# Folding projection weights head by head on 64 rows of TensorE, in a decoder block on one core

## The reference

```python
x = x + mixer(layernorm(x))          # gated mixer, 256 wide, a causal filter over the 4 batches
x = x + xattn(layernorm(x), ctx)     # cross attention, 16 heads of 64, relu features of size 128
x = x + ffn(layernorm(x))            # 8 experts, each token goes to 2 of them

def xattn(query_input, source_input, Wq, Wk, Wv, Wo, proj):
    q = einsum('bld,dhk->blhk', query_input, Wq)
    k = einsum('bld,dhk->blhk', source_input, Wk)
    v = einsum('bld,dhk->blhk', source_input, Wv)
    qp = relu(einsum('blhd,md->blhm', q, proj) / sqrt(128)) + 1e-3
    kp = relu(einsum('blhd,md->blhm', k, proj) / sqrt(128)) + 1e-3
    kvs = einsum('blhm,blhd->bhmd', kp, v)
    num = einsum('blhm,bhmd->blhd', qp, kvs)
    den = einsum('blhm,bhm->blh', qp, kp.sum(axis=1))
    return einsum('blhd,hdk->blk', num / den[..., None], Wo)
```

## Time and profile before

| | us |
|---|---|
| median of 3 runs | 284.33 |
| lowest and highest | 284.23, 286.0 |
| the profiled execution, its own time | 283.41 |
| span of the profiled execution | 281.6 |

### The profile page before, as it was taken

The page is one execution under the profiler, slowest core; times in us unless marked ns, Lnnn a source line. Parts: engine busy times, 40 slices in busy tenths (PEclk is TensorE's granted clock), DMA queues, the critical chain, the costliest instruction groups (busy, mean ns, idle before and its releaser), DMA issues.

```text
span 281.6 us, 5724 instructions
## 1 busy us (share of the span) xinstructions
PE 250.0 (89%) x1697; PEld 214.2 (76%) x1697; DVE 190.6 (68%) x713; ACT 163.9 (58%) x343; POOL 123.7 (44%) x183
## 2 busy tenths in 40 slices
PE   7799999999999999999998999896799989999700
PEld 4558677676888999879887998775699989999600
DVE  4868759587868888998889889899367222232215
ACT  3566466564677777667766776661156656565400
POOL 5648999651001002047103701270236777777710
PEclk9999999999999999999999999999699999999975
DMA  7999999930012000001000100019557579984147
GB/s 208 276 240 202 204 205 195 198 47 2 0 58 94 0 0 3 1 21 48 9 3 17 52 11 3 9 55 280 155 160 198 160 211 281 354 256 130 43 181 266
DMA packets 38446, 34.05 MB, mean 121 GB/s; under 512 B 3581, under 2 KB 31234, under 8 KB 38288
## 3 DMA queue, kind: packets, MB, share of 16 engines
q1 hardware_dynamic: 35312, 28.96, 43.4%
q0 software_dynamic: 2272, 4.24, 4.4%
q10 hardware_dynamic: 832, 0.49, 0.6%
HBM read 19.80 MB, written 14.32 MB: 121 GB/s over the span
## 4 chain that ended last, share of the span: by engine, by line
PE 59%; DVE 20%; DMA 8%; SPq 5%; issue 4%; POOL 2%; ACT 1%; DVEq 0%; POOLq 0%; ACTq 0%
PE bank L1250 10%; PE num L1175 10%; DVE X L913 8%; PE bank L1136 5%; PE num L1260 5%; PE num L1114 5%; DMA xb<-dispatched 3%; PE num L245 3%; PE num L247 3%; PE bank L245 3%; PE num L246 3%; PE bank L1078 3%; PE bank L246 2%; PE bank L247 2%; DMA wo_sb<-in_wo 2%
## 5 line engine op out<-in xcount | busy, mean ns | idle before, releaser
L913 DVE SCALAR_TENSOR_TENSOR X<-num,rden,X 128x128 f32<-128x128 f32 x256 | 72.1, 344 | 6.6
L1175 PEld LDWEIGHTS num<-kvw_sb,q 128*128 128x128 f32 x512 | 65.9, 190 | 12.0 <-ACT q L574 5.7
L1175 PE MATMUL num<-kvw_sb,q 128*128 128x130 f32 x512 | 68.7, 277 | 3.6 <-DVE X L913 3.6
L657 ACT ACTIVATE relu_z<-bank 128x512 f32<-128x512 f32 x64 | 38.1, 596 | 21.6 <-PE bank L247 21.5
L537 POOL DMA_INDIRECT dispatched<-rows,slot_i x32 | 31.3, 977 | 40.4 <-DVE rows L979 31.6
L557 POOL DMA_INDIRECT expert_out<-yo,xb x39 | 38.1, 977 | 20.1 <-ACT yo L686 11.3
L1013 DVE TENSOR_TENSOR hid<-bank,silu_g 128x256 f32<-128x256 f32 x39 | 16.5, 424 | 41.2 <-ACT silu_g L682 41.2
L574 ACT ACTIVATE q<-relu_z 128x512 f32<-128x512 f32 x64 | 40.4, 632 | 6.7 <-DVE acc L832 0.8
L1250 PE MATMUL bank<-xT,wgu_sb 128*128 128x128 f32 x312 | 43.3, 284 | 0.2 <-ACT xT L574 0.2
L1250 PEld LDWEIGHTS bank<-xT,wgu_sb 128*128 128x128 f32 x312 | 39.8, 200 | 0.5 <-issue 0.5
L245 PE MATMUL bank<-y2T_hi,feat_hi 128*128 128x512 f32 x64 | 30.4, 475 | 0.2
(11 more groups left out here) (170 smaller groups left out, 403.2 us busy)
## 6 DMA issues: line engine op xcount, KB each, us to landing
wgu_sb<-in_wgu SPq DMA_DIRECT2D x39, 256.0 KB, 3.4
dispatched<-pad_row SPq DMA_DIRECT2D x3, 2795.0 KB, 32.6
xb<-dispatched SPq DMA_DIRECT2D x39, 65.0 KB, 3.5
y_back<-expert_out SPq DMA_DIRECT2D x4, 512.0 KB, 4.9
wd_sb<-in_wd SPq DMA_DIRECT2D x1, 1024.0 KB, 4.7
out<-X SPq DMA_DIRECT2D x4, 256.0 KB, 2.4
X<-in_x SPq DMA_DIRECT2D x3, 256.0 KB, 5.9
expert_out<-yo,xb POOLq DMA_INDIRECT x39, 3.5
```

The costliest lines, as they stand in the source:

```text
L657: a.activation(relu_z[:, k % 2, :], z_bank[k % 2], ACT.Relu).then_inc(relu_done, 1)
L913: v.scalar_tensor_tensor(tile_of(n, t), banks[:, t // 2, t % 2, 0:P], rden[:, h % 2, t:t + 1], tile_of(n, t), ALU.mult, ALU.add).then_inc( ...
L1175: nc.tensor.matmul(num[:, 2 * (h % 2) + t // 2, HA * (t % 2):HA * (t % 2 + 1)], q[:, h % 4, part], kvw_h, start=True, stop=True).then_inc( ...
```

## The change

The pairs are taken apart. `projT_sb` and `wo_sb` become 128 columns wide and have no zero blocks, so that the four memsets and `apart` go. Each head is folded by a matmul of its own, on rows 0 to 63 or 64 to 127 (`row_half`), with 128 moving columns. The host lays out wk, wv, wq and wo anew: the heads of group g lie on rows 0 to 63 when g is even and on rows 64 to 127 when g is odd. In the folds of the start PE goes over two groups at once, in turns from the one half of the rows to the other and from one bank to the other. In the batches' `project` all four heads of a group lie on the same half of the rows and go to the same bank. wo is loaded by two transfers, with 512 contiguous floats to a row.

```diff
-            projT_sb = sa("projT_sb", [P, 2 * M])
+            projT_sb = sa("projT_sb", [P, M])
-            wo_sb = sa("wo_sb", [P, H // 2, 2 * P])
+            wo_sb = sa("wo_sb", [P, H // 2, P])
+        def row_half(g):
+
+            return slice(DH * (g % 2), DH * (g % 2 + 1))
             for i in range(2):
                 part = slice(G * i, G * (i + 1))
                 sp.dma_start(wv_sb[:, part, :], wv[:, part, :]).then_inc(ld_wvo[i], 16)
-                sp.dma_start(wo_sb[0:DH, part, 0:P], wo[0:DH, part, :]).then_inc(ld_wvo[i], 16)
-                sp.dma_start(wo_sb[DH:P, part, P:2 * P], wo[DH:P, part, :]).then_inc(ld_wvo[i], 16)
+                sp.dma_start(wo_sb[:, part, :], wo[:, part, :]).then_inc(ld_wvo[i], 16)
             act.dma_start(projT_sb[0:DH, 0:M], projT).then_inc(ld_proj, 16)
-            act.dma_start(projT_sb[DH:P, M:2 * M], projT).then_inc(ld_proj, 16)
+            act.dma_start(projT_sb[DH:P, 0:M], projT).then_inc(ld_proj, 16)
-            v.memset(projT_sb[0:DH, M:2 * M], 0.0).then_inc(apart, 1)
-            v.memset(projT_sb[DH:P, 0:M], 0.0).then_inc(apart, 1)
-            v.memset(wo_sb[0:DH, :, P:2 * P], 0.0).then_inc(apart, 1)
-            v.memset(wo_sb[DH:P, :, 0:P], 0.0).then_inc(apart, 1)
             def project(ps, w, g):
-                for i in range(G // 2):
-                    last = nc.tensor.matmul(ps[:, 2 * M * i:2 * M * (i + 1)], w[:, G // 2 * g + i, :], projT_sb[:, :],
-                                            start=True, stop=True)
+                for i in range(G):
+                    last = nc.tensor.matmul(ps[:, M * i:M * (i + 1)], w[row_half(g), G * (g // 2) + i, :],
+                                            projT_sb[row_half(g), :], start=True, stop=True)
                 return last
             pe.wait_ge(ld_proj, 32)
-            pe.wait_ge(apart, 2)
-            for g in range(NG):
-                pe.wait_ge(ld_wk[g], 16)
-                project(fold_bank[g], wk_sb, g).then_inc(wk_full, 1)
-            pe.wait_ge(apart, 4)
-            for g in range(NG):
-                pe.wait_ge(ld_wvo[g // 2], 48)
-                pe.wait_ge(wk_lo_done, g + 1)
-                for i in range(G // 2):
-                    last = nc.tensor.matmul(fold_bank[g][:, 2 * P * i:2 * P * (i + 1)], wv_sb[:, G // 2 * g + i, :],
-                                            wo_sb[:, G // 2 * g + i, :], start=True, stop=True)
-                last.then_inc(wvo_full, 1)
+            for a in range(2):
+                for i in range(G):
+                    if i % 2 == 0:
+                        pe.wait_ge(ld_wk[2 * a + i // 2], 16)
+                    for g in (2 * a, 2 * a + 1):
+                        fold = nc.tensor.matmul(fold_bank[g][:, M * i:M * (i + 1)], wk_sb[row_half(g), G * a + i, :],
+                                                projT_sb[row_half(g), :], start=True, stop=True)
+                        if i == G - 1:
+                            fold.then_inc(wk_full, 1)
+            for a in range(2):
+                pe.wait_ge(ld_wvo[a], 32)
+                pe.wait_ge(wk_lo_done, 2 * a + 2)
+                for i in range(G):
+                    for g in (2 * a, 2 * a + 1):
+                        fold = nc.tensor.matmul(fold_bank[g][:, P * i:P * (i + 1)], wv_sb[row_half(g), G * a + i, :],
+                                                wo_sb[row_half(g), G * a + i, :], start=True, stop=True)
+                        if i == G - 1:
+                            fold.then_inc(wvo_full, 1)
```

More of the change, by code:

```diff
@@ L190, in decoder_kernel @@
         ld_wq = sem("ld_wq")
-        warm_set, apart = sem("warm_set"), sem("apart")
+        warm_set = sem("warm_set")
         ld_bias, ld_small, ld_biaso, ld_woa, ld_wd = map(sem, ("ld_bias", "ld_small", "ld_biaso", "ld_woa", "ld_wd"))
@@ L1294, with halves @@
     coef = np.concatenate([w["attn_zero"], w["attn_pos"][:, :NB - 1]], axis=1)
+    def halves(a):
+        return a.reshape(2, 2, G, DH, P).transpose(1, 3, 0, 2, 4).reshape(P, H // 2, P)
     arrays = {
@@ L1303 @@
         "coef": np.repeat(coef, MHD, axis=0).reshape(2, P, NB).transpose(1, 0, 2),
-        "wk": w["xattn_Wk"].transpose(1, 2, 0).reshape(H // 2, P, P).transpose(1, 0, 2),
-        "wv": w["xattn_Wv"].transpose(1, 2, 0).reshape(H // 2, P, P).transpose(1, 0, 2),
-        "wq": w["xattn_Wq"].transpose(1, 2, 0).reshape(H // 2, P, P).transpose(1, 0, 2),
-        "wo": w["xattn_Wo"].reshape(H // 2, P, P).transpose(1, 0, 2),
+        "wk": halves(w["xattn_Wk"].transpose(1, 2, 0)),
+        "wv": halves(w["xattn_Wv"].transpose(1, 2, 0)),
+        "wq": halves(w["xattn_Wq"].transpose(1, 2, 0)),
+        "wo": halves(w["xattn_Wo"]),
         "projT": w["xattn_proj"].T,
```

## The result

| | before | changed |
|---|---|---|
| median, us | 284.28 (4 runs) | 288.27 (4 runs) |
| lowest and highest | 284.21, 286.0 | 286.93, 290.12 |
| the profiled execution, its own time | 283.41 | 290.12 |
| its span | 281.6 | 288.4 |

The ratio is 1.0118, with a 95% interval from 1.0071 to 1.0165. Two later calls on chips of the same speed gave 1.0127 [1.0076, 1.0179] and 1.0155 [1.0094, 1.0216]. The change makes the kernel slower by 1.2 to 1.6%, 3.4 to 4.4 us. The forecast was 285.1 us, with a range to 287.2: wrong.

A forecast was written before the change was run, and what follows sets the result against it. The prediction took PE to bound the kernel from 13.44 us on, with the norm's work as late at the start. Start -0.05, wq matmuls +0.16 and row changes +0.64 gave +0.75: 284.33 + 0.75 = 285.1 us, range 283.6 to 287.2.

The forecast's parts named there:

- PE must empty before the change ... I take 0.08: Folds of wq: each change between whole array and half its rows costs 0.08 us, 8 x 0.08 = 0.64.
- The second rival: Folds of wq: PE empties at each change, 8 x 0.16 = 1.3 us, giving 285.7 us; chance 0.22.
- the join that cost nothing: Lower bound for a change of rows: kvw to the fold of wq today, 24.90 + 0.90 = 25.80, without loss.
- The +0.04 for the matmuls themselves: Each fold of wq: eight records, 0.90 us in place of 0.86; four times, +0.16 us.
- The memsets ... worth nothing: Start: the memsets ran while DVE waited for x, to 6.28 us, so dropping them gains nothing.
- x ... lands before wo does: Start: x of batch 0, issued by ACT, lands at 6.28 us, ahead of wo, and the change shortens nothing there.
- The first is there at about 8.8: Start: wo's first half lands at about 8.8 us in place of 9.26, through quicker transfers, 0.4 us each half.
- Against it: on the whole array loading runs beside the matmuls: Folds of wq: argument that weight loads stay hidden, since PE and PEld are both busy today.
- the third rival: Folds of wq: weight loads on the same half no longer hidden, +3.6 us, giving 288.7 us; chance 0.08.
- half way between the emptying and the dear end, 287.2: Top of the forecast range, set between PE emptying at each change (285.7 us) and 287.8 us.
- the dear end: Folds of wq: each change costs a full PE restart, 0.42 us, +3.5 us in all, giving 287.8 us; chance 0.05.
- The median lies 0.9 us above that execution: Whole kernel: carries the forecast from the profiled execution's 283.41 us over to the median, giving 284.33 + 0.75.

The follow-up runs named there:

- again: The changed kernel with nothing altered, run once more for a second profile: 288.53 us, ratio 1.0127 to the kernel before.
- twice: The changed kernel with each fold of wq split into two heads, kvw(6), then the other two; on a slower chip 320.32 against 314.93 us, ratio 1.0185.
- two_queues2: The changed kernel with wq folded in pairs on 128 rows, SP issuing proj ahead of wk, ACT issuing x first: 283.12 us, ratio 0.9956 to the kernel before.

## Why the prediction was wrong

- **"PE must empty before the change ... I take 0.08".** The term that was mis-sized, and the first step that failed. The changes between the whole array and half of it cost 0.19 us each, 8 x 0.19 = 1.5 us in place of 0.64. The second rival was right on this term, its 0.16 a little low; its time, 285.7, was not reached either. The middle between two rows was no argument: the join that cost nothing was between 77 and 128 rows, which turned out to be no change of that kind. The +0.04 for the matmuls themselves was right (4 x 0.04).
- **"The memsets ... worth nothing".** The step that failed in kind. Their run time was worth nothing, but with four instructions fewer in DVE's list two gaps of 0.46 us appear in attention: +0.8 on the path. No row of the kernel before could show this.
- **"x ... lands before wo does", at 6.28 us.** I took one execution's landing for the program's. It varies from 6.3 to 8.7 us in kernels with the old start. The mechanism was right, and it held more strongly than I had it: the norm's line of work bounds the start of the changed kernel (`context(1)` followed the landing of x by 8.7 us in all four profiles), and so hides the earlier folds. A late x also holds DVE's copies of the first folds: PE began the folds of wv at 10.74 in the first profile and at 9.21 in `again`, waiting for `key_lo` both times, and not at 8.8.
- **"The first is there at about 8.8".** In the changed kernel's four profiles the halves of wo landed at 8.7 to 9.4 and at 10.1 to 10.8 us, in five with the old start at 9.2 to 10.7 and at 11.4 to 12.8. So they do come earlier, about as forecast (8.8 and 10.6), but not by the pace alone: the last transfer is issued at 4.2 in place of 6.0, which the forecast put at nothing.
- **"Against it: on the whole array loading runs beside the matmuls".** Right; the third rival, dear weight loads on the same half, didn't come: a fold's pace stays at 0.11 us a record between the changes.
- **What the sum lacked.** The changes (1.5), the matmuls (0.16) and the gaps (0.8) are 2.5 us, as measured from `context(1)` to the end of attention. The 3.4 to 4.4 us of the ratios hold one or two more. In the profiles the late stall is the place where more is lost, and why is not settled. Single executions of one kernel spread by more than that (the kernel before ran from 282.4 to 286.6 on one chip).
- **"half way between the emptying and the dear end, 287.2".** The middle between 285.7 and 287.8 is 286.75. With either bound the measured 288.3 lies outside.
- **"The median lies 0.9 us above that execution".** Fair then; the changed kernel's profiled execution lay 1.9 us above its median, so a difference of two profiled spans (6.8 us) overstates the change by 2.8 us.

## What to carry to other kernels

Taking zero blocks out of a matmul of two stacked heads saved no time on TensorE by itself here (eight records at 0.11 us in place of four at 0.215). What saves is turning from one half of the rows to the other with each matmul, and what costs is every entry into and exit from the half array, 0.19 us, so such matmuls belong together and not one group at a time between full ones. Before removing work in front of a wait, list the other lines of work that end at the same instant (here x, moments, POOL, `xn`) and take several profiles of when they end. And an edit of instructions that are hidden can still change what the rest of that engine's program does: compare intervals far behind it. Last, compare paces only at the same clock, and look from where on a trace has a record of it.

## What the runs showed of the hardware

- Matmuls in turns on the two halves of the rows run at once. The folds of wv in the changed kernel's first profile, 16 records in 1.16 us, where 8 records on the whole array had taken 1.97:

```profile
10.74 1.16 PE L1064 MATMUL bank<-wo_sb,wv_sb 64*128 64x128 f32 x16 [2.01 <-DVE key_lo L704]
```

Two records start every 0.112 us, which is 0.056 a record. The Trainium skill, "TensorE: Matmul & The Clock Gate", Part 3, says that matmuls on different row groups overlap; this trace agrees.
- The same folds also go at half that pace, two records in 0.213 us, and it is the clock that decides. In `twice` the first half of them ran at a granted clock of 1.00, the second at 0.50 (chain, then stretches):

```profile
10.28 1.16 PE bank L1064 x16
11.48 2.02 PE num L1064 x16
```

```profile
10.00:11.00 1.00, 0.72 (x12) 0.75 (x14) 1.00 (x3) 0.00 (x0) 0.92 (x2) 1.00 1.19 336
12.00:13.00 1.00, 1.00 (x12) 1.00 (x12) 0.93 (x2) 0.53 (x2) 0.92 (x2) 0.50 1.09 323
```

- At the start of a kernel the clock column misleads. A trace's first record of the granted clock lies at 4.16 us in the kernel before, at 9.24 in the changed one and at 14.38 in `two_queues2`; ahead of it the views print 1.00. In all twenty traces the folds go at the slow pace ahead of that first record, and where it says 0.50, and at the fast pace elsewhere: 0.106 and 0.056 us a record in turns, 0.427 and 0.216 for 256 columns on the whole array. So the folds of wk in the changed kernel (2.08 us for the 16 that took 1.16 in `again`) and both folds of wv in `two_queues2` (2.08 and 1.71 us on the chain) ran at the lower clock too; that is read from the paces, since no record of the clock covers them. Why the first record comes so late in some executions is open.
- A gap of 0.46 us on DVE comes and goes with the length of its program (seven profiles with, thirteen without).
- x of batch 0 landed at 7.20 and 8.70 us in two executions of the kernel before on one chip, and at 6.28 on another, while the steps from there to `context(1)` took 8.67 or 8.68 us in all four profiles of the changed kernel.
